# Feed-forward units of an attention and feed-forward kernel: down projections in two banks by turns, and one more halving of the squares on VectorE

## The reference, cut to what matters

```
x = x + layernorm(attention(layernorm(x)))
x = x + layernorm(feed_forward(layernorm(x)))

feed_forward(x):
    gate, up = split(x @ W_gate_up^T)      # 2 x 1024 features; weights made ternary by groups of 64
    h  = silu(gate) * up                   # 1024 hidden features
    hn = h * rsqrt(mean(h * h) + eps)      # one factor a token
    return hn @ W_proj^T                   # 256 features; weights made ternary
```

## Time and profile before

| | |
|---|---|
| median of 3 runs | 1160.51 us (1160.51 to 1162.78) |
| profiled execution | 1161.09 us |
| its span, first to last instruction | 1159.3 us |
| TensorE busy / weight loads | 1076.3 us (93%) / 1008.8 us (87%) |
| VectorE busy | 874.5 us (75%) |
| ScalarE busy | 845.0 us (73%) |
| GpSimd busy | 914.9 us (79%) |
| granted TensorE clock, mean | 0.99 |

### The profile page before, as it was taken

One profiled execution on the slowest core, in us unless ns is written; L12 is line 12 of the kernel. 1 busy time (PEld: TensorE's weight loads), 2 busy tenths in 40 slices (PEclk: granted clock), 3 DMA queues, 4 the chain that ended last, 5 costly groups with the idle time before them and its releaser, 6 DMA issues.

```text
span 1159.3 us, 26824 instructions
## 1 busy us (share of the span) xinstructions
PE 1076.3 (93%) x7990; PEld 1008.8 (87%) x7990; DVE 874.5 (75%) x2875; ACT 845.0 (73%) x2326; POOL 914.9 (79%) x845
## 2 busy tenths in 40 slices
PE   5799899989999999999899989999999899999996
PEld 4688898889888988898889888998988789999995
DVE  4578978897888779878987797878785656566563
ACT  2677777777777777787777777777777866666663
POOL 2687888797979797979798889888888647776774
PEclk8999999999999999999999999999999999999998
DMA  8260102010211111111011111111031000000000
GB/s 283 78 197 29 56 29 75 18 64 19 74 31 52 42 60 37 46 55 47 28 55 55 38 28 55 37 38 47 29 105 34 1 1 20 19 18 18 18 28 28
DMA packets 35192, 57.77 MB, mean 50 GB/s; under 512 B 3120, under 2 KB 15984, under 8 KB 34800
## 3 DMA queue, kind: packets, MB, share of 16 engines
q1 hardware_dynamic: 32912, 53.56, 14.9%
q10 hardware_dynamic: 2176, 3.15, 0.8%
HBM read 50.66 MB, written 9.18 MB: 52 GB/s over the span
## 4 chain that ended last, share of the span: by engine, by line
POOL 43%; issue 28%; PE 22%; ACT 3%; DVE 2%; DMA 1%; POOLq 1%; ACTq 0%; DVEq 0%; SPq 0%
POOL arena L526 13%; POOL arena L536 11%; POOL arena L547 9%; PE psum L835 8%; PE psum L852 6%; POOL arena L558 5%; PE psum L658 4%; POOL X L517 2%; ACT arena L1079 1%; PE psum L872 1%; POOL arena L503 1%; PE psum L753 1%; DVE pt_split L1318 1%; POOL arena L496 1%; PE psum L887 1%
## 5 line engine op out<-in xcount | busy, mean ns | idle before, releaser
L558 POOL TENSOR_TENSOR arena<-arena 128x768 f32<-128x768 f32 x128 | 188.2, 1470 | 106.7 <-DVE arena L1305 100.6
L526 POOL TENSOR_TENSOR arena<-arena,tables 128x512 f32<-128x512 f32 x128 | 174.4, 1363 | 17.5 <-ACT arena L979 17.5
L1318 DVE SCALAR_TENSOR_TENSOR pt_split<-psum,vh_col,pt_split 128x256 fp32r<-128x256 f32 (+1 forms) x512 | 187.3, 406 | 0.0
L753 PE MATMUL psum<-arena 128*128 128x256 f32 x512 | 157.6, 389 | 28.8 <-POOL arena L536 27.0
L536 POOL TENSOR_TENSOR arena<-arena 128x512 f32<-128x512 f32 x128 | 175.8, 1374 | 10.7 <-POOL arena L526 1.1
L990 ACT ACTIVATE arena<-arena 128x256 f32<-128x256 f32 x256 | 129.9, 507 | 74.4 <-DVE arena L1295 69.1
L547 POOL TENSOR_TENSOR arena<-arena 128x512 f32<-128x512 f32 x128 | 164.5, 1285 | 6.2 <-DMA arena<-kh_rows 6.2
L1280 DVE TENSOR_TENSOR arena<-psum,tables 128x512 f32<-128x512 f32 x128 | 86.1, 673 | 100.7 <-PE psum L658 95.2
L978 ACT ACTIVATE arena<-psum 64x512 f32<-64x512 f32 x128 | 76.1, 595 | 105.2 <-DVE arena L1280 105.1
L658 PE MATMUL psum<-wo_hi,o_hi 128*128 128x256 f32 x512 | 152.7, 298 | 0.0
L658 PE MATMUL psum<-xt_hi,wq_hi 128*128 128x256 f32 x512 | 146.9, 287 | 0.0
(11 more groups left out here) (161 smaller groups left out, 3511.5 us busy)
## 6 DMA issues: line engine op xcount, KB each, us to landing
arena<-kh_rows SPq DMA_DIRECT2D x128, 256.0 KB, 3.3
out<-spare SPq DMA_DIRECT2D x16, 256.0 KB, 2.1
arena<-w_rows SPq DMA_DIRECT2D x6, 512.0 KB, 4.3
X<-L_attn_Wout SPq DMA_DIRECT2D x1, 2048.0 KB, 14.8
X<-L_attn_x SPq DMA_DIRECT2D x1, 2048.0 KB, 9.5
w_rows<-L_ffn_w_gate_up ACTq DMA_DIRECT2D x4, 512.0 KB, 8.0
arena<-L_attn_Wq SPq DMA_DIRECT2D x1, 1536.0 KB, 10.4
X<-L_attn_x SPq DMA_DIRECT2D x1, 1536.0 KB, 15.7
```

The costliest lines, as they stand in the source:

```text
L526: nc.gpsimd.tensor_tensor(swap, swap, spread, ALU.mult).then_inc(q_sined, 1)
L558: nc.gpsimd.tensor_tensor(tb, tb, r.unsqueeze(3).to_broadcast([P, HP, 3, P]), ALU.mult).then_inc(p_ready, 1)
L753: nc.tensor.matmul(sj[:, 0:2 * P], q[:, j, P:N], kt[:, j, :], start=True, stop=True, skip_group_check=True)
L1318: last = nc.vector.scalar_tensor_tensor(pt_lo[p % 2][:, o], b[:, i], vh[:, t, h:h + 1], pt_hi[p % 2][:, o].bitcast(F32), ALU.mult, ALU.sub ...
```

## The change

A second bank, `Z_BANK = [bank[4], bank[6]]`, is used by turns for the down projection: bank 4 was used in attention only. Reads of the bank (`stats_z`, `norm_z`) go by the unit's bank, and `down` of unit u waits for norm_z of unit u - 2. The wait for the last copy of attention's output out of bank 6 goes from unit 0 to unit 1, the first that uses that bank.

`sum_squares` gets a second add: after the halving from four blocks of 256 tokens to two, VectorE waits for it and adds the second block to the first. TensorE then sums one block for each tile of tokens, not two.

```diff
+        Z_BANK = [bank[4], bank[6]]
...
-                        if isinstance(u, int) and u == 0:
+                        if isinstance(u, int) and u == 1:
                             pe.wait_ge(y_copied, STEPS)
-                        at_least(pe, z_norm, u * NT)
+                        at_least(pe, z_norm, (u - 1) * NT)
...
-                            last = nc.tensor.matmul(Y_BANK[:, t * E:(t + 1) * E], part[:, f, t * P:(t + 1) * P],
+                            last = nc.tensor.matmul(Z_BANK[i][:, t * E:(t + 1) * E], part[:, f, t * P:(t + 1) * P],
...
-                        for f in range(FC):
-                            last = nc.tensor.matmul(O_BANK[:, t:t + 1], squares[i][:, f, t * P:(t + 1) * P], ones[:, :],
-                                                    start=t == 0 and f == 0, stop=f == FC - 1, skip_group_check=True)
+                        last = nc.tensor.matmul(O_BANK[:, t:t + 1], squares[i][:, 0, t * P:(t + 1) * P], ones[:, :],
+                                                start=t == 0, stop=True, skip_group_check=True)
...
                 dve.wait_ge(h_added, u * 2 + 2)
+                nc.vector.tensor_tensor(a, a, b, ALU.add).then_inc(h_halved, 1)
+                a, b = squares[i][:, 0, :], squares[i][:, 1, :]
+                dve.wait_ge(h_halved, u + 1)
                 nc.vector.tensor_tensor(a, a, b, ALU.add).then_inc(h_summed, 1)
```

More of the change, by code:

```diff
@@ L272, in sandwich_kernel @@
             sem(k) for k in ("gate_ready", "up_ready", "gate_silu", "h_ready", "h_squared", "ht_hi_done", "ht_lo_done"))
-        h_added, h_summed, sum_ready, z_floored, z_ready = (
-            sem(k) for k in ("h_added", "h_summed", "sum_ready", "z_floored", "z_ready"))
+        h_added, h_halved, h_summed, sum_ready, z_floored, z_ready = (
+            sem(k) for k in ("h_added", "h_halved", "h_summed", "sum_ready", "z_floored", "z_ready"))
         z_stats, z_aggr, z_eps, z_neg, z_inv, z_biased, z_norm, res_done = (
@@ L1078, in norm_z @@
                 for t in range(NT):
-                    nc.scalar.activation(zn[i][:, t, :], Y_BANK[:, t * E:(t + 1) * E], ACT.Identity, bias=z_bias[:, t:t + 1],
+                    nc.scalar.activation(zn[i][:, t, :], Z_BANK[i][:, t * E:(t + 1) * E], ACT.Identity, bias=z_bias[:, t:t + 1],
                                          scale=z_rstd[:, t:t + 1]).then_inc(z_norm, 1)
@@ L1422, in stats_z @@
                 for t in range(NT):
-                    nc.vector.bn_stats(z_stat[:, t, :], Y_BANK[:, t * E:(t + 1) * E]).then_inc(z_stats, 1)
+                    nc.vector.bn_stats(z_stat[:, t, :], Z_BANK[i][:, t * E:(t + 1) * E]).then_inc(z_stats, 1)
                 dve.wait_ge(z_stats, u * NT + NT)
```

## The result

The changed kernel took 1174.23 us (median of 4 runs, 1173.5 to 1175.17), against 1160.80 (4 runs, 1160.51 to 1162.78) of the kernel before beside it: a ratio of the means of 1.0113 [1.0095 to 1.013] (ratios below are of means too). It is slower, by 13.4 us; 1173.0 was forecast, in a range of 1160 to 1179.

What follows compares the result with a forecast made beforehand. A ScalarE and VectorE loop of 13.32 us a step, without TensorE releases, was taken to bound the kernel. Terms summed to +12.5 us on the profiled 1161.09: 1173.6, or 1173.0 as median; range 1160 to 1179.

Steps and rivals of the forecast that it cites:

- entry: Down 0 to 2: part of the add's delay falls into ScalarE's existing waits; +2.4 us in all.
- the end: After high_hidden 3 of the last unit: down projection no longer held by norm_z of unit 14; -3.0 us, within 1 us.
- ten like steps: Down 3 to 12: each step longer by 1.44 us, +14.4 us in all.
- down 13: Step of down 13: +1.44 us for the add, -2.3 from high_hidden 1 to 3, mainly waits for TensorE gone.
- down 14: Step of down 14: +1.44 us for the add, -1.9 from high_hidden 1 to 3, taken as 4.7 us.
- The second add held by split_hidden: VectorE, before multiply 1: new add waits for GpSimd's split_hidden at the port; +1.44 us a step, between 0.44 and 1.71.
- the part on rows 6: Earlier trace pair: GpSimd's residual, waiting since add_squares, went before the dependent sum_squares, which took 1.67 us, 0.98 more.
- the second rival: VectorE's second add slips in before GpSimd: 0.44 us a step, -1.0 us in all, 1160 us; chance 0.12.
- the prediction's 0.53 for 512: VectorE add of 512 elements: estimated 0.53 us of its 0.69 grows with length.
- The banks worth 0 in the steps: Down projection: the second bank removes TensorE's wait for norm_z, worth 0 in steps whose period is ScalarE's and VectorE's.
- third rival: TensorE, idle some 2.3 us a step, falls to half clock: 0.7 us a step, 8 in all, 1181 us; chance 0.05.
- First rival: Wait before each down projection: TensorE sets the step, 13.32 to 12.45 us; -13.7 us in all, 1147 us; chance 0.09.

Runs made afterwards that it cites:

- the fastest kernel: The whole change, with the second add moved behind multiply 1 and add_squares of chunks 0 and 1 behind multiply 3, against the kernel before: 1149.86 us, ratio 0.9896.

## Why the prediction was right, step by step

The mechanism was right and most terms held. Measured between norm_z's (the entry from the first up-projection matmul, the end to the end of the span), against those predicted:

| term | predicted | measured |
|---|---|---|
| entry, to norm_z of down 3 | +2.4 | 54.71 - 51.56 = +3.15 |
| ten like steps | +14.4 | 146.61 - 133.26 = +13.35 |
| down 13 | +1.44 - 2.3 = -0.86 | 12.43 - 13.22 = -0.79 |
| down 14 | +1.44 - 1.9 = -0.46 | 11.76 - 11.82 = -0.06 |
| end | -3.0 | 12.74 - 15.53 = -2.79 |
| sum | +12.5 | +12.86 |

- **The second add held by split_hidden, +1.44 a step.** Right in kind: 1.39 us long, ending 0.28 after split_hidden, as the part on rows 6 said; the move behind multiply 1 and the cut to 8 columns show that it is this wait. Steps alternate; every second one gained 1.42. The others gained 1.30 (one of them 1.05): before, multiply 1 in those steps waited 0.18 us for GpSimd's split_hidden, and that wait is now hidden behind the add. The step of down 9 is one of the first kind, and the prediction priced all ten by it (VectorE's timeline before, step of down 10):

```profile
1083.57 0.69 DVE L1389 TENSOR_TENSOR arena<-arena,psum 128x512 f32<-128x512 f32 x1 [0.18 <-POOL wo_lo L564]
```

- **Which rule of the port.** The Trainium skill, "SBUF — State Buffer", section "Who interferes with whom", calls the port that VectorE and GpSimd share an exclusive lock. This case agrees: split_hidden takes 1.73 us with the new add beside it, 1.74 without, and the add of 8 columns ends 0.02 us after it. Sharing would have stretched both; the second rival (0.44 us a step) is out.
- **The add by itself.** 0.42 us undisturbed, taken as 0.41; 0.69 - 0.42 = 0.27 for 256 elements is also what the prediction's 0.53 for 512 gives. (By the formula for an fp32 add in the Trainium skill, "VectorE: DVE Perf Modes", section on the TRN2 errata, it is an estimated (256 + 151)/0.96 ns = 0.42 us; the row agrees.)
- **The banks worth 0 in the steps.** Right: 13.32 against 13.33 us. Also right that they give most at the end, where the add's loss hides it.
- **Entry.** "The 1 us that the residual cost there before is not met again" was wrong. GpSimd's residual, its add to X, is met again and delays sum_squares first, then split_hidden the new add: 0.7 us more than the sum has (timelines of GpSimd, VectorE and ScalarE of the kernel after, step of down 2; before):

```profile
974.92 1.75 POOL L518 TENSOR_TENSOR X<-X,arena 128x512 f32<-128x512 f32 x1
976.63 1.71 POOL L565 TENSOR_TENSOR wo_lo<-arena,wo_hi 128x512 fp32r<-128x512 f32 x1
...
975.55 1.66 DVE L1402 TENSOR_TENSOR arena<-arena 128x512 f32<-128x512 f32 x1
977.25 1.37 DVE L1405 TENSOR_TENSOR arena<-arena 128x256 f32<-128x256 f32 x1
...
980.33 0.63 ACT L1057 ACTIVATE wo_hi<-arena 128x512 fp32r<-128x512 f32 x1 [4.27 <-DVE arena L1389]
```

- **Down 14** saved 0.4 us less than I took off for waits on TensorE, which the sum has "now far ahead" from down 13 on. In down 14 it wasn't: from high_hidden 1 (1152.81) to 3 (1157.91) it took 5.10 us instead of 4.7, and 0.3 of that is multiply 2, which waited for TensorE's up projection until 1155.27 while activate 2 had ended at 1154.38 + 0.58 = 1154.96 (VectorE's timeline after). This and the entry are balanced by the alternate steps: that the sum is nearer than its terms is luck.

```profile
1155.27 0.69 DVE L1389 TENSOR_TENSOR arena<-arena,psum 128x512 f32<-128x512 f32 x1 [0.89 <-PE psum L836]
```

- **The end** went as worked out (VectorE's timeline; before): the sums of squares wait for GpSimd's add of x, the new add for nothing, and the floor (the epsilon with the token's factor) for 4 matmuls.

```profile
1160.88 1.66 DVE L1402 TENSOR_TENSOR arena<-arena 128x512 f32<-128x512 f32 x1
1162.57 0.42 DVE L1405 TENSOR_TENSOR arena<-arena 128x256 f32<-128x256 f32 x1
1163.69 0.16 DVE L1421 TENSOR_SCALAR arena<-psum 128x2 f32<-128x2 f32 x1 [0.70 <-PE psum L872]
```

- **TensorE's clock** (third rival): the idle time came in three pieces, not two, and the granted clock stayed at 1.00, 2.4 GHz, through the step (window of the kernel after, columns as above):

```profile
1076.10:1090.90 14.80, 13.20 (x107) 12.59 (x106) 9.51 (x18) 8.98 (x19) 9.54 (x14) 1.00 0.05 18
```

- **First rival**, TensorE sets the step: not here, but nearly so once both held adds are off ScalarE's loop. Its 12.45 us was right for TensorE's own work (12.39: eight matmuls take 0.79 us, four take 0.34 where the squares are ready). It left out that the sums then wait for the second add, which makes 12.67 of it.

## What to carry to other kernels

An added instruction costs what its place in the queue makes it cost: the same add was worth 1.33, 0.21 or 0 us a step at three places of one queue, a few instructions apart. Look for the other engine's instruction that is already waiting for the shared port when the added one is issued, and put work that nobody needs soon behind the instruction that another engine waits for. Removing work from an engine that has slack, TensorE here, gains nothing until the loop that sets the step has been shortened to its length. Even then the work that was moved can take some back: of the 0.45 us that four matmuls fewer save here, 0.19 was left in the fastest kernel, as the sums had to wait for the add in their place.

## What the runs showed of the hardware that wasn't expected

- Between two VectorE adds that follow each other by 0.03 us (1079.83 to 1079.86), a waiting GpSimd operation takes the port: the second add is held for the whole of it.
- A tiny GpSimd operation (128x2) is held as well: 0.70 us instead of 0.18 behind a VectorE add of 0.68 (banks, with add_squares moved).
- Sums by a column of ones: 8 matmuls take 0.79 us in the chain, 4 take 0.34 where the squares are ready and 0.60 where their weight loads wait for the second add.
- Three waits of TensorE in each step, of 0.3 to 0.8 us mostly, left its clock at 1.00 (kernel after); one of 3.02 us with nothing done was followed by 0.50 (second add alone).
